# First-layer expert weights of a two-layer mixture: the half-precision split moved from VectorE to GpSimd

## The reference, cut to what matters

```python
x = x + tanh(g_xattn[0]) * L0_xattn(layernorm(x), ctx, ...)      # additive attention, 16 heads
x = x + tanh(g_ffn[0])   * L0_ffn(layernorm(x), W_router, b_router, W1, b1, W2, b2)
x = x + tanh(g_xattn[1]) * L1_xattn(layernorm(x), ctx, mask, Wq, Wk, Wv, Wo)   # softmax attention
x = x + tanh(g_ffn[1])   * L1_ffn(layernorm(x), router_w, w1, w2)

def L0_ffn(x, ...):
    logits = x @ W_router + b_router
    top_vals, top_idx = top_k(logits, 2)
    ...
    for e in range(8):
        h = relu(x @ W1[e] + b1[e])          # W1[e] is 128 x 512
        y = h @ W2[e] + b2[e]
        out += y * w[:, e]
```

## Time and profile before

| what | us |
|---|---|
| median of 3 runs | 760.57 |
| lowest and highest run | 759.96, 770.91 |
| span of the profiled execution | 865.4 |
| busy in it: PE, DVE, ACT, POOL | 578.2, 418.2, 234.8, 340.6 |

### The profile page before, as it was taken

One profiled execution on the slowest core, in us unless ns is written; L12 is line 12 of the kernel. 1 busy time (PEld: TensorE's weight loads), 2 busy tenths in 40 slices (PEclk: granted clock), 3 DMA queues, 4 the chain that ended last, 5 costly groups with the idle time before them and its releaser, 6 DMA issues.

```text
span 865.4 us, 17483 instructions
## 1 busy us (share of the span) xinstructions
PE 578.2 (67%) x5468; PEld 451.0 (52%) x5469; DVE 418.2 (48%) x1454; ACT 234.8 (27%) x411; POOL 340.6 (39%) x424
## 2 busy tenths in 40 slices
PE   2588765233598988882798887667572047999970
PEld 1256544011387877772454665545351026888860
DVE  5774777663232323234884668266173811222225
ACT  1220011220043343343521554233241111222220
POOL 6122046476045454555400000612515665555660
PEclk9786957655799999997699997567555578999995
DMA  7801001131222222232754353232204112222219
GB/s 209 225 25 37 13 26 40 35 125 53 72 71 67 62 65 62 69 119 68 231 172 125 97 151 105 75 99 50 57 8 141 37 49 76 69 69 73 75 43 291
DMA packets 73195, 76.52 MB, mean 88 GB/s; under 512 B 12984, under 2 KB 61368, under 8 KB 73064
## 3 DMA queue, kind: packets, MB, share of 16 engines
q1 hardware_dynamic: 58504, 50.98, 21.3%
q0 software_dynamic: 10224, 22.40, 8.4%
q10 hardware_dynamic: 4400, 2.26, 0.9%
HBM read 46.15 MB, written 29.34 MB: 87 GB/s over the span
## 4 chain that ended last, share of the span: by engine, by line
PE 35%; DVE 20%; issue 16%; another core or an unknown queue 11%; POOL 8%; DMA 4%; ACT 3%; SPq 2%; DVEq 1%; ACTq 0%; POOLq 0%
PE PS L758 31%; POOL ys L528 5%; DMA work<-ys 2%; DVE XN L1340 2%; DVE work L1314 2%; POOL xs L517 2%; DVE stats L1319 2%; DVE work L1729 2%; DVE X L1314 1%; DVE rtmp L1314 1%; POOL turn L526 1%; PE PS L939 1%; PE PS L1089 1%; DVE mv L1322 1%
## 5 line engine op out<-in xcount | busy, mean ns | idle before, releaser
L517 POOL DMA_INDIRECT xs<-pack,adr_i x80 | 79.1, 988 | 235.3 <-ACT pack L1164 154.2
L758 PE MATMUL PS<-w,work 128*128 x1152 | 145.7, 280 | 14.0 <-ACT work L1212 6.5
L528 POOL DMA_INDIRECT ys<-work x144 | 141.0, 979 | 34.1 <-issue 34.1
L758 PEld LDWEIGHTS PS<-w,work 128*128 128x128 f32 x1152 | 135.5, 193 | 25.0 <-issue 24.0
L758 PE MATMUL PS<-work,w1h 128*128 128x256 f16 x576 | 101.9, 278 | 22.7 <-issue 14.1
L1212 ACT ACTIVATE work<-PS,b 128x256 f32<-128x256 f32 x160 | 62.6, 477 | 117.1 <-PE PS L758 93.1
L1314 DVE TENSOR_TENSOR work<-PS,work 128x256 f32<-128x256 f32 (+3 forms) x82 | 33.0, 404 | 121.7 <-issue 75.5
L758 PE MATMUL PS<-work 97*64 97x256 f16 (+5 forms) x608 | 75.5, 318 | 17.2 <-DVE work L1446 10.9
L758 PE MATMUL PS<-work,w1l 128*128 128x256 f16 x288 | 79.9, 278 | 0.6 <-issue 0.6
L758 PEld LDWEIGHTS PS<-work 97*64 97x64 f16 (+2 forms) x608 | 57.8, 165 | 28.4 <-DVE work L1446 13.5
L758 PEld LDWEIGHTS PS<-work,w1h 128*128 x576 | 53.5, 99 | 31.7 <-issue 25.8
(11 more groups left out here) (261 smaller groups left out, 877.3 us busy)
## 6 DMA issues: line engine op xcount, KB each, us to landing
work<-xs SPq DMA_DIRECT2D x132, 65.0 KB
work<-ys SPq DMA_DIRECT2D x12, 512.0 KB, 5.9
k_parts<-work SPq DMA_DIRECT2D x24, 128.0 KB
w<-k_parts SPq DMA_DIRECT2D x8, 384.0 KB
work<-k_parts SPq DMA_DIRECT2D x32, 96.0 KB
work<-q_parts SPq DMA_DIRECT2D x8, 384.0 KB
work<-q_parts SPq DMA_DIRECT2D x32, 96.0 KB
ys<-work POOLq DMA_INDIRECT x144
```

Source lines behind the costliest of these rows:

```text
L517: g.indirect_dma_start(xs[l], bass.IndirectOffsetOnAxis(adr_i[:, k, T:T + 1], 0), pack_of(l, c)[:, s, k, :].bitcast(U32), None)\
L528: g.indirect_dma_start(ys[l], bass.IndirectOffsetOnAxis(xin[:, q, u, :].bitcast(U32)[:, D:D + 1], 0), yrow[:, q, u, :], None).then_inc(ff[ ...
L758: return t.matmul(o, lhsT, rhs, start=start, stop=stop, skip_group_check=True)
```

## The change

The split moves to POOL in both layers. There it is three instructions, each of which waits for the one before: scale the raw weights in place, copy them to `w1h`, subtract `w1h` from the scaled weights into `w1l`. In the first layer all eight splits stand in POOL's loop over the chunks, each behind its `x_plus`, and the load of expert `e + 2` follows the split of `e`. In the second layer all eight stand behind POOL's sums and ahead of its scatters. SP issues two `w1_load` per chunk in chunks 0 to 3 and none in 4 to 7. DVE gets one new wait, for `w1_lo[0]`, ahead of a memset that overlaps the raw buffer.

```diff
-            "split 0/load 6/load 7/heads 0 0/split 1/logits 0 1/exp 0 1/keys 0/key_logits 0/weights 0 1/split 2/pool 0 1/"
...
+            "load 6/load 7/heads 0 0/logits 0 1/exp 0 1/keys 0/key_logits 0/weights 0 1/pool 0 1/"
...
+            def split_w1(l, raw, e):
+                o = slice(e * FF, (e + 1) * FF)
+                pool.wait_ge(w1_in[l][e % 2], 16 * (e // 2 + 1))
+                then(g.tensor_scalar(raw[:, e % 2, :], raw[:, e % 2, :], WSCALE, None, ALU.mult))
+                then(g.tensor_copy(w1h[:, o], raw[:, e % 2, :]))
+                g.tensor_tensor(w1l[:, o], raw[:, e % 2, :], w1h[:, o], ALU.subtract).then_inc(w1_lo[l], 1)
+
             pool.wait_ge(fold_in, 4)
             g.tensor_copy(X[:, :, D:DE], bc(crow_lg, 1, NT))
             for e in range(E):
                 pool.wait_ge(xn_done, e + 1)
                 g.tensor_tensor(X[:, tiles(e), 0:D], ...).then_inc(x_plus, 1)
-                if e < 2:
-                    continue
-                pool.wait_ge(w1_lo[0], e - 1)
-                g.dma_start(w1raw[:, e % 2, :], A["w1_0"][e]).then_inc(w1_in[0][e % 2], 16)
+                split_w1(0, w1raw, e)
+                if e + 2 < E:
+                    pool.wait_ge(w1_lo[0], e + 1)
+                    g.dma_start(w1raw[:, e % 2, :], A["w1_0"][e + 2]).then_inc(w1_in[0][e % 2], 16)
...
+            for c in range(NC):
+                pool.wait_ge(q_out[c], Q_STORED)
+            for e in range(E):
+                split_w1(1, w1raw1, e)
             for c in range(NC):
                 if c < NC // 2:
                     for s in range(CT_TILES):
...
-                w1_load(c)
+                if c < E // 2:
+                    w1_load(2 * c)
+                    w1_load(2 * c + 1)
...
-            def split_w1(l, raw, e):
-                dve.wait_ge(w1_in[l][e % 2], 16 * (e // 2 + 1))
-                o = slice(e * FF, (e + 1) * FF)
-                link(v_.tensor_scalar(w1h[:, o], raw[:, e % 2, :], WSCALE, None, ALU.mult))
-                v_.scalar_tensor_tensor(out=w1l[:, o], in0=raw[:, e % 2, :], scalar=WSCALE, in1=w1h[:, o],
-                                        op0=ALU.mult, op1=ALU.subtract).then_inc(w1_lo[l], 1)
...
-                elif step == "split":
-                    split_w1(0, w1raw, m)
...
             dve.wait_ge(x1_done, NC)
+            dve.wait_ge(w1_lo[0], E)
             v_.memset(kmask[:, 0, :, :, :], 0.0).then_inc(k_blank, 1)
...
-                k = chunk_at(g, 3)
-                if k == 0:
-                    for c in range(NC):
-                        dve.wait_ge(q_out[c], Q_STORED)
-                if k is not None:
-                    split_w1(1, w1raw1, k)
```

## The result

The changed kernel takes 773.55 us (median of four runs, 771.92 to 779.26) beside 763.39 for the kernel before (four runs, 759.96 to 770.91): a ratio of 1.0159, 95% interval 1.0121 to 1.0197. The medians are 10 us apart; the ratio, which is taken without runs in the slower of the chip's two states, gives 12 us, between 9 and 15. The forecast was 758.5, a little faster, and its range ended at 767. The splits of both layers were moved, and not only those of the first, which the title names.

What follows compares the result with a forecast made beforehand. No engine was taken as full; a split counts only where DVE holds the chain. Terms: -6.4 for splits, +3.3 for collisions, +1.0 for loads, sum -2.1 us, so 760.57 becomes 758.5 us, range 751.5 to 767.

Steps and rivals of the forecast that it cites:

- The price of a split on DVE: On DVE in both layers: one split takes 1.07 us, sixteen take 17.1 us of DVE's 418.2.
- What the change takes away: DVE's splits on the chain: six, three per layer, at 1.07 us, gain 6.4 us; the ten others give nothing.
- the reservation in the text: Last split of each layer: without profiler or stall, POOL's scatters may hide it, making it worth nothing.
- "lower end" of 4.3: Gain from splits taken off DVE's chain if the last split of each layer is hidden: 4.3 us instead of 6.4.
- The price of a split on POOL: POOL, both layers: three instructions, 1.28 us subtraction, 0.8 each for scale and copy; 2.9 us, between 2.1 and 3.8.
- Rival (d): Second layer: POOL splits over 4.6 us hold SP at chunks 2 and 3, maxima late; +1.9, 762.5 us; chance 0.08.
- Rival (b): Both routers' ends set by POOL's scatters and PE's lead, the rest lost to collisions: nothing gained, 760.6 us; chance 0.10.
- "what POOL does to DVE": POOL's subtractions hold DVE 1.1 us per hit: one at layer 0's norm, two at layer 1's choice; 3.3 us, 0 to 11.
- Rival (c): Scale and copy also hold DVE, whole splits at a norm and group 0's choice: +6.5, 767.1 us; chance 0.15.
- The doubled loads: Layer 1, chunks 0 to 3: second load delays query blocks and maxima, counted once at 1.0 us, 0 to 3.
- The two hits forecast in layer 1's choice: Layer 1, router group 0: POOL's splits 6 and 7 fall on DVE's choice, two hits, 2.2 us.

Runs made afterwards that it cites:

- mixed: Kernel before, with POOL doing layer 0's splits 5 to 7 behind its last `x_plus` and all of layer 1's, loads paired: 766.26 us, ratio 1.0048.
- reorder: Kernel before, all splits still on DVE, layer 0's splits 5, 6 and 7 moved to other places in DVE's order: 763.5 us, ratio 1.0001.
- l0_pool: Kernel before with only the first layer's half of the change: 773.27 us, ratio 1.0156.
- apart: Kernel before with layer 1's doubled loads, DVE splitting the two of a pair one step from each other: 763.92 us, ratio 1.0018.
- best: Kernel before with reorder's layer 0 and the second layer's half of the change: 766.83 us, ratio 1.0047.
- early: Changed kernel, but in layer 0 only splits 0 and 1 stay among the `x_plus`, the others behind all of them: 769.73 us, ratio 1.0122.
- nosub: Changed kernel without the subtraction in layer 0's splits, the low part filled with zeros once at the start: 774.23 us, ratio 1.0176.
- ctrl: Kernel before, unchanged, run and profiled again; its profile is the second profile of before: 759.91 us in one run.
- l1_pool: Kernel before with only the second layer's half of the change, paired loads included: 761.97 us, ratio 0.9987.
- l1_pairs: Kernel before with layer 1's loads doubled, DVE splitting both of a pair in one place: 766.04 us, ratio 1.0046.
- l1_pool_b: The same kernel as l1_pool, against the kernel before on another chip: 764.4 us, ratio 1.003.
- l1_pairs_b: The same kernel as l1_pairs, against the kernel before, on one chip with l1_pool_b: 768.18 us, ratio 1.0068.

## Why the prediction was wrong

**The price of a split on DVE was right.** 1.07 us, seen as a step of PE's wait three times over.

**What the change takes away was too much.** Six splits were counted as on the chain. Two of layer 0's stand behind the first scatter, where POOL is the bound; the reservation in the text covered this for split 7 and not for split 6. In layer 1 the chain of the second profile of before has splits 3 and 5, and not 7: POOL scatters without a pause from 561.20 to 600 us and beyond. These are its pieces:

```profile
487.64 0.35 DVE w1h L1353
...
526.81 0.35 DVE w1h L1353
```

The chain of the stalled profile had given the eighth a piece at 646.23. So three splits were left, 3.2 us, below the "lower end" of 4.3, and of these three the one of layer 0, split 5, is too small for the times of mixed and reorder to show.

**The price of a split on POOL was nearly right.** 37.49 to 39.75 + 1.15 is 3.4 us, forecast 2.9 between 2.1 and 3.8; the scale is 1.50, the cast 0.61. POOL's splits of layer 0 end at 74.7 (forecast 65 to 80), those of layer 1 at 488, ahead of the scatters, and SP is not held. Rival (d) is out. Rival (b), nothing gained, is what the second layer's half came to by itself.

**The failing step is "what POOL does to DVE" in layer 0.** It read: "In the first layer POOL's splits fall between 30 and 80, where PE leads, except for the norm of chunks 2 and 3 at 37 us with its row of small dependent instructions: one hit, 1.1 us." Four things in it were off. The norm there is that of chunks 4 and 5; the one of 2 and 3 is at 20 to 27. There is a second norm, of chunks 6 and 7, at 47 to 53, which was not counted. At each, POOL is busy nearly all the time, so not one instruction is held but three or four of the ten small ones, and the pass of eight pieces with them. And "PE leads" was taken from a stretch of 60 us, in which one line of PE had 60% of the chain; up to 39.91 us PE stands still for 8.56 us, waiting for this norm. (At the second norm PE does lead in the second profile of before, whose chain has PE from 46.38 to 51.09; in the changed kernel's chain DVE's norm stands there.) The term comes out as follows, from the two timelines. From the first copy back: 50.53 - 44.81 = 5.7 us at the first norm, the small row 3.5 longer (35.88 to 41.25 against 36.85 to 38.75), the pass 3.5, the soft weights 0.9, less 2.1 for an earlier start and a shorter wait for PE. From there to the second copy: 76.12 - 64.60 - 5.7 = 5.8 more, where DVE was even relieved of three splits. Together 11.5 where 1.1 stood. The first part is firm: in ten profiles of kernels that are unchanged up to there the first copy comes at 44.1 to 44.9 us. The second is less so: the second copy comes at 64.6 to 67.6 us in these, and at 76.1 and 76.9 in the changed kernel and l0_pool, so the sum is between 8.6 and 12.3 us. That 11.5 meets the 12 of the timed runs so closely is in part the luck of the profile it was compared with.

**Rival (c) named the mechanism and was too small by the same step.** It priced one split at one norm, 2.9 us, and reached 767.1. Priced at both norms, with the rows of the profile after, the same mechanism gives most or all of the loss. Its threshold, that DVE is held on the chain for more than 5 us in sum, is passed by the first norm alone.

The Trainium skill, SBUF — State Buffer, "Who interferes with whom", says more than the sentence that the prediction weighed: the port pair that GpSimd and VectorE share is a lock that the one who comes first keeps for its whole instruction, and copies, casts and scalings of VectorE can take it as well, while reductions never do. The traces agree in kind. In the changed kernel a reduction from 69.18 us took 0.69 us beside an `x_plus` from 69.30 to 70.56, as it does without; the norm's scaling pass took 5.62 against 2.14. On "whole instruction" they agree for two-input passes (39.92 + 1.01 ends with the subtraction, 39.75 + 1.15) and for the cast (39.09 + 0.59 with 39.05 + 0.61), and not for the scale: the instruction of 37.62 + 0.84 was through at 38.46, and the scale, 37.49 + 1.50, at 38.99. On who comes first the row at 35.88 doesn't fit: DVE had started 0.38 us ahead of the `x_plus` with which it ended.

**The doubled loads**, forecast at 1.0 between 0 and 3, are neither confirmed nor refused: apart stands at +1.4 us with an interval of -1.3 to +4.1. PE's wait ahead of the same kind of matmul is 1.33 us in the changed kernel (at 475.21), not 2.8. The two hits forecast in layer 1's choice were one, 1.15 us.

**What stays open.** The sum of the terms is now 8.6 to 12.3 for layer 0 and about 0 for layer 1, beside 12 measured (9 to 15). Why mixed and best stand 0.5% above the kernel before isn't settled; both hold the second layer's half, whose own two measurements were 0.9987 and 1.003. That early loses more than its first norm's 5.0 us (49.79 against 44.81 at the first copy) may come from PE's clock, by the stretches above; that was read, not tested: no run changed the clock alone, and the unchanged kernels themselves take anything from 19.8 to 23.5 us from the first copy to the second, where early takes 24.4. How much the load issues of POOL hold DVE beside its passes was not tested either. No version beat the kernel before.

## What to carry to other kernels

Work moved to GpSimd can be paid by VectorE where both touch SBUF at once; ask for each place, with its start and end, what VectorE does there that has two SBUF inputs or scales within SBUF, and multiply by how many of its instructions find GpSimd busy. In this case GpSimd was busy for 93% of the stretch with the first norm (7.46 of 8 us), and VectorE's dependent row of tiny instructions and its scaling pass took 5.4 and 5.6 us there instead of 1.9 and 2.1; the same work 20 us later cost 2.7 us instead of 12 in all. Read "who leads" in a window as short as the piece in question: a share of 60% over 60 us hid 8.6 us in which PE did nothing. And take the difference of two profiles only after seeing how far profiles of one kernel differ.

## What the runs showed of the hardware

A GpSimd scale of f32 in place (128x512, one input) takes 1.50 us, longer than the two-input `x_plus` of 1.28 and than a two-input subtraction with f16 output, 1.15; the cast from f32 to f16 takes 0.61. GpSimd waits in its turn: the same scale took up to 1.99 us beside the soft weights of DVE. A GpSimd fill, which reads nothing, holds DVE too: in nosub DVE's scaling pass, begun at 24.62 us, ended at 30.18, and the fill of 128x4096 f16 at 30.10.

The kernel before is not as steady as its layout suggests. In kernels whose first 100 us hold the same instructions the first scatter came at 113.90, 114.00, 116.72, 116.80, 118.74 and 121.17 us (ctrl, l1_pool, l1_pairs, apart, l1_pool_b, l1_pairs_b), and at 118.55 in the first profile of before. The changed kernel and l0_pool, alike up to there, have 125.35 and 130.46. From 60 to 68 us PE's granted clock was 1.00 in ctrl and 0.79 in mixed, whose POOL had done nothing new by then. That is 7 us of spread from the first 120 us alone, and it is why a single pair of profiles can't show an effect of 2 us on the time; for that many timed runs are needed.
